# Attention stages of a fused transformer kernel: a fourth slot, row maxima and outputs turned through the score banks, outputs copied out by ScalarE and multiplied by GpSimd

## The reference

```python
x = x + _L1_attn_ref(_layernorm(x), ...)     # stage 4
    scores = jnp.einsum('bhqd,bhkd->bhqk', q, k) * scale
    attn = jax.nn.softmax(scores, axis=-1)
    out = jnp.einsum('bhqk,bhkd->bhqd', attn, v)
    return jnp.einsum('bld,ed->ble', out, wo) + bo
...
x = x + _L3_attn_ref(_layernorm(x), ...)     # stage 10
    att = (jnp.einsum('bhid,bhjd->bhij', q, k) + bias[None]) * (1.0 / math.sqrt(D))
    att = jax.nn.softmax(jnp.where(causal, att, -jnp.inf), axis=-1)
```

## Time and profile before

| | us |
|---|---|
| median of three runs | 3656.55 (3642.74 to 3657.66) |
| the profiled execution, its own time | 3656.68 |
| its span in the trace | 3654.9 |
| stage 4, about | 1074 to 1828 |
| stage 10, about | 2824 to 3410 |

### The profile page before, as it was taken

One profiled execution on the slowest core, in us unless ns is written; L12 is line 12 of the kernel. 1 busy time (PEld: TensorE's weight loads), 2 busy tenths in 40 slices (PEclk: granted clock), 3 DMA queues, 4 the chain that ended last, 5 costly groups with the idle time before them and its releaser, 6 DMA issues. The chain is left out here.

```text
span 3654.9 us, 60936 instructions
## 1 busy us (share of the span) xinstructions
PE 3204.0 (88%) x23629; PEld 1672.5 (46%) x23629; DVE 2528.7 (69%) x5604; ACT 1906.4 (52%) x3456; POOL 997.7 (27%) x858
## 2 busy tenths in 40 slices
PE   4678876798979999999889998989899799898899
PEld 3212223565652333333256666657676223232677
DVE  8787769777758888888487774363534688884433
ACT  2232222577757888888767773313222256677221
POOL 0245552667720000000096670000300211211100
PEclk9779978899987999999999998989999689899899
DMA  1000000211115000000021111000300500000100
GB/s 50 9 1 1 0 0 12 72 26 39 32 35 185 2 1 1 1 1 1 1 79 30 34 29 28 2 26 1 93 1 16 157 1 30 33 1 1 45 1 12
DMA packets 72854, 99.82 MB, mean 27 GB/s; under 512 B 11748, under 2 KB 51688, under 8 KB 72360
## 3 DMA queue, kind: packets, MB, share of 16 engines
q1 hardware_dynamic: 72568, 95.92, 8.9%
HBM read 62.81 MB, written 19.45 MB: 23 GB/s over the span
## 5 line engine op out<-in xcount | busy, mean ns | idle before, releaser
L1959 ACT ACTIVATE AR<-ps 128x1024 f32<-128x1024 f32 (+2 forms) x756 | 718.0, 995 | 194.8 <-PE ps L1860 122.9
L2042 DVE TENSOR_REDUCE AR<-ps 128x1 f32<-128x512 f32 x1056 | 671.7, 684 | 83.2 <-PE ps L1829 82.5
L1860 PE MATMUL ps<-AR 32*128 32x512 bf16 (+3 forms) x4992 | 610.2, 379 | 9.4 <-ACT AR L1959 5.8
L1829 PE MATMUL ps<-AR 32*128 32x512 bf16 (+3 forms) x1664 | 446.0, 400 | 41.0 <-DVE AR L2039 19.9
L1877 PE MATMUL ps<-AR 128*32 128x512 f32 (+3 forms) x3328 | 441.0, 603 | 4.0 <-ACT AR L1964 3.5
L2462 PEld LDWEIGHTS ps<-AR 128*128 128x128 f32 x3072 | 364.8, 193 | 60.5 <-issue 47.3
L2621 DVE SCALAR_TENSOR_TENSOR X<-ps,AR,X 128x128 f32<-128x128 f32 x512 | 143.6, 344 | 345.0 <-PE ps L2462 344.6
L2462 PE MATMUL ps<-AR 128*128 128x128 f32 x3072 | 364.9, 276 | 0.0
L1860 PEld LDWEIGHTS ps<-AR 32*128 32x128 bf16 x4992 | 227.2, 95 | 191.4 <-ACT AR L1959 47.6
L2437 PE MATMUL ps<-XT,AR 128*128 128x512 f32 x672 | 307.7, 594 | 0.0
L1829 PEld LDWEIGHTS ps<-AR 32*128 32x128 bf16 x1664 | 114.9, 92 | 396.0 <-DVE AR L2042 196.1
(11 more groups left out here) (324 smaller groups left out, 5711.2 us busy)
## 6 DMA issues: line engine op xcount, KB each, us to landing
AR<-AR SPq DMA_DIRECT2D x124, 128.0 KB, 2.3
AR<-in_c_rot SPq DMA_DIRECT2D x64, 128.0 KB, 2.2
AR<-in_L3f_w SPq DMA_DIRECT2D x30, 256.0 KB, 5.3
rows_KA<-AR SPq DMA_DIRECT2D x32, 128.0 KB, 2.4
AR<-scr_bias SPq DMA_DIRECT2D x32, 128.0 KB, 3.1
AR<-in_L2f_w SPq DMA_DIRECT2D x30, 128.0 KB, 2.8
AR<-rows_KC SPq DMA_DIRECT2D x7, 512.0 KB, 6.2
rows_QA<-AR SPq DMA_DIRECT2D x24, 128.0 KB, 2.4
```

The source lines that it names most:

```text
L1829: e.matmul(g.bank[b][:, 0:w], QA[rows, q, 128 * i:128 * i + 128], KA[rows, q, 512 * first:512 * first + w], start=way != "kept", stop=True ...
L1860: t = e.matmul(g.bank[h][:, lo:512], K[32 * h:32 * h + 32, q, 128 * kt:128 * kt + 128], Q[32 * h:32 * h + 32, q, queries], start=y == 0, s ...
L1959: e.activation(dst[:, :, lo:512], src[:, :, lo:512], ACT.Exp, scale=self.scale).then_inc(*s.up("exp" if u else "left", k, i, *((1,) if u e ...
L2042: e.tensor_reduce(o, g.bank[b][:, 0:w], AXX, ALU.max).then_inc(*s.up("reduced", k, n, h, st, kc))
```

## The change

1. `RC` gets a fourth slot in both stages; L1989 (and L2005 in stage 4) then waits for the part four before. Two of its slots serve later as `OS`.
2. In stage 4 only round 0 keeps the paired maxima. Head 1 of rounds 1 to 15 is reduced block by block like the others: 120 negated products, 120 copies of ACT and 120 paired reductions of DVE go, 240 plain reductions come. GpSimd negates once instead of 16 times. Within a "max" of round 0 the two products of one head now follow each other.
3. In stage 4 the maxima of a step stand in pairs: heads 2 and 3 ahead of the scores, heads 0 and 1 behind them. In stage 10 their order stays.
4. "max_rows" goes to bank 0 ahead of the scores u = 0 of a step, "finish" to bank 2 ahead of the scores u = 1. Both leave the ring.
5. The turned outputs are copied out of bank 2 by ACT ("finish", into `OS`); one step later DVE takes the reciprocal from there and GpSimd multiplies ("inverse").
6. In stage 10 the values' projections move from between the maxima of round 0 into the making of the parts.

```diff
-        self.RC = ar.f32(3, 512)
+        self.RC = ar.f32(4, 512)
+        self.OS = self.RC[:, 0:2, :]
...
-        if self.causal or (n and h != 1):
+        if self.causal or n:
             return "alone"
...
-    def plan_rows_max(self, n):
-        b = self.spare()
+    def plan_rows_max(self, n, b):
         self.plan.append(("max_rows", n, b, self.hold(b, ("max_row", n))))
 
-    def plan_finish(self, n):
-        b = self.spare()
-        self.plan.append(("finish", n, b, self.hold(b, ("finished", n))))
+    def plan_finish(self, n, b):
+        self.plan.append(("finish", n, b, self.hold(b, ("moved_out", n))))
...
+            if causal and x < len(self.parts) and not j:
+                self.plan_rows(c)
...
-        side = [0, 1, 2, 3]
+        side = [] if causal else [0, 1, 2, 3]
...
-            if self.rows_due:
-                self.plan_rows_max(self.rows_due.pop(0))
             self.plan_closed()
-        while self.rows_due:
-            self.plan_rows_max(self.rows_due.pop(0))
...
+            else:
+                order = [x[y] for y in range(3) for x in pairs if y < len(x)]
+                slots = [order[0:1], [], order[1:], []]
             for u in range(2):
                 for x in slots[u]:
                     self.plan_max(*x)
+                if u == 0 and self.rows_due:
+                    self.plan_rows_max(self.rows_due.pop(0), 0)
+                if u and finish_due:
+                    inverse_due += [(i + 1, finish_due[0])]
+                    self.plan_finish(finish_due.pop(0), 2)
...
+            if what == "finish":
+                n, b, _ = x
+                e.wait_ge(*s.at("o_turned", k, n))
+                if n > 1:
+                    e.wait_ge(*s.at("finished", k, n - 2))
+                e.activation(self.OS[:, n % 2, :], g.bank[b], ACT.Copy).then_inc(*s.up("ot", k, n, "out"))
...
-                if y > 2:
-                    e.wait_ge(*s.at("third", k, *self.parts[y - 3]))
+                if y > 3:
+                    e.wait_ge(*s.at("third", k, *self.parts[y - 4]))
...
+            if what == "inverse":
+                n = x[0]
+                gr, qc = self.rounds[n]
+                v = self.OS[:, n % 2, :].rearrange("p (i h d) -> p i h d", i=4, h=4)
+                e.wait_ge(*s.at("inverse", k, n))
+                e.tensor_tensor(self.AO[:, 4 * qc:4 * qc + 4, 32 * gr:32 * gr + 32].rearrange("p i (h d) -> p i h d", h=4),
+                                v[:, :, :, 0:8], bc(self.RD[:, n % 2, :, :], [128, 4, 4, 8], 3), ALU.mult).then_inc(
+                                    *s.up("finished", k, n))
```

More of the change, by code:

```diff
@@ L1454, in allocate @@
             self.KEPT = ar.f32(6, 512)
[L1455 removed]
+            self.NQ = ar.bf16(512)
         self.PB = ar.f32(4, 1024)
@@ L1608, in lay_plan @@
             pairs = [self.next_max(half, goal, 3) for half in (1, 0)]
-            order = [x[y] + (2 * x[y][1] + z,) for y in range(3) for x in pairs if y < len(x) for z in range(2)]
-            slots = [[x for y, x in enumerate(order) if 4 * y // max(4, len(order)) == z] for z in range(4)]
+            if causal:
+                order = [x[y] + (2 * x[y][1] + z,) for y in range(3) for x in pairs if y < len(x) for z in range(2)]
+                slots = [[x for y, x in enumerate(order) if 4 * y // max(4, len(order)) == z] for z in range(4)]
+            else:
+                order = [x[y] for y in range(3) for x in pairs if y < len(x)]
+                slots = [order[0:1], [], order[1:], []]
             for u in range(2):
@@ L1632, in lay_plan @@
                 self.plan_max(*x)
+            if inverse_due and inverse_due[0][0] == i:
+                self.plan.append(("inverse", inverse_due.pop(0)[1]))
             self.plan_closed()
@@ L1636, in lay_plan @@
         for n in finish_due + [15]:
-            self.plan_finish(n)
+            self.plan_finish(n, 2)
+            inverse_due += [(0, n)]
+        for _, n in inverse_due:
+            self.plan.append(("inverse", n))
     def wait_left(self, e, s, old):
@@ L1656, in wait_left @@
                 e.wait_ge(*s.at("max_row", k, *key))
-            if what == "finished":
-                e.wait_ge(*s.at("finished", k, *key))
+            if what == "moved_out":
+                e.wait_ge(*s.at("ot", k, *key, "out"))
             if what == "left":
@@ L1823, in tensor @@
                     if way == "kept":
-                        e.matmul(g.bank[b], self.NQ[rows, n % 2, 128 * st:128 * st + 128], KA[rows, q, chunk(kc)],
+                        e.matmul(g.bank[b], self.NQ[rows, 128 * st:128 * st + 128], KA[rows, q, chunk(kc)],
                                  start=True, stop=False, skip_group_check=True)
-                for h, b, old in heads:
-                    way, rows = self.way(n, h, kc), slice(32 * h, 32 * h + 32)
                     first = kc + 1 if way == "kept" else kc - 1 if way == "met" else kc
@@ L1911, in scalar @@
                     e.wait_ge(*s.at("rc_pool", k, c, j))
-                    e.activation(piece, self.RC[:, y % 3, :], ACT.Copy).then_inc(*s.up("piece", k, c, j, 1))
+                    e.activation(piece, self.RC[:, y % 4, :], ACT.Copy).then_inc(*s.up("piece", k, c, j, 1))
                 else:
@@ L2091, in gpsimd @@
         for what, *x in self.plan:
-            if what == "max" and not self.causal:
-                n, st, kc, heads = x
-                if n + st + kc == 0 and heads[0][0] == 2:
-                    self.turn_sign(e, s, 0)
-                if heads[0][0] == 2 and st == 3 and kc == (0 if n else 2) and n < 15:
-                    self.turn_sign(e, s, n + 1)
             if what == "compact" and self.causal:
                 y, c, j, _, _, _ = x
-                rest = self.RC[:, y % 3, :]
+                rest = self.RC[:, y % 4, :]
                 e.wait_ge(*s.at("rotated", k, c, j, 1))
@@ L2105, in gpsimd @@
                 e.wait_ge(*s.at("piece", k, c, j, 2))
-                e.tensor_tensor(self.P[:, j, 2, chunk(c)], self.RC[:, y % 3, :], self.P[:, j, 1, chunk(c)],
+                e.tensor_tensor(self.P[:, j, 2, chunk(c)], self.RC[:, y % 4, :], self.P[:, j, 1, chunk(c)],
                                 ALU.subtract).then_inc(*s.up("third", k, c, j))
+                if not self.causal and y == len(self.parts) - 1:
+                    e.wait_ge(*s.at(self.max_rows_in(*self.rounds[0], False), k))
+                    e.tensor_scalar(self.NQ, self.rows["QA"][:, 0, chunk(self.rounds[0][1])], -1.0, 1.0, ALU.mult,
+                                    ALU.mult).then_inc(*s.up("minus", k))
             if what == "close":
@@ L2648, in gpsimd @@
             root(e, s, g, k + 1, c)
-VECTOR = ("added", "below", "bias_rows", "biased", "centered", "closed", "final", "finished", "gate_added", "gated",
+VECTOR = ("added", "below", "bias_rows", "biased", "centered", "closed", "final", "gate_added", "gated",
           "hidden", "lifted_scores", "moments", "norms", "over", "p_odd", "product",
@@ L2658 @@
           "weights", "xh", "xt", "yt")
-GPSIMD = ("b2_added", "half", "last", "m_parts", "minus", "near_biased", "paired", "power", "product_pool", "rc_pool",
+GPSIMD = ("b2_added", "finished", "half", "last", "m_parts", "minus", "near_biased", "paired", "power", "product_pool", "rc_pool",
           "rest", "root", "rstd", "scaled_table", "summed", "third", "unit", "x_biased")
```

42 lines of the change are left out of this document (14 added, 28 removed).

## The result

| | before | after |
|---|---|---|
| median, us | 3657.11 (3642.74 to 3661.61, 4 runs) | 3759.70 (3753.42 to 3765.89, 4 runs) |
| span of the profiled execution | 3654.9 | 3751.6 |
| ratio after to before | | 1.0287, 95% interval 1.0254 to 1.0321 |

The changed kernel is slower by 103 us where +44 was forecast. I cut the two traces at the same places and took the difference of each piece (after less before, us): stage 4, up to its last projection, +24.8; stages 5 to 9, which nobody touched, and the start of stage 10 up to its first scores, -7.5, of which the start alone is -10.1 and the rest +2.7; the rounds of stage 10, from the first load of the values' weights to the last, **+78.4**; the end +1.4. With -0.4 between the first scores of stage 10 and its first values that is the 96.7 by which the spans differ. So nearly all of the surprise is in the rounds of stage 10.

A forecast was written before the change was run, and what follows sets the result against it. PE was taken as the bound, stretched by waits on the ring of three banks, where the fourth maximum waits for the first's reduction. Stage 4 +33 and stage 10 +11 on 3656.7 gave 3701 us; 8-in-10 range 3645 to 3765.

The forecast's parts named there:

- The plain steps: Stage 4 steps without turnings: every one 2.49 us instead of some at 2.61, saving 1.0 us a round.
- Turning steps of stage 4: Stage 4: row-maxima step 5.01 us against 3.79, output step 3.98 against 3.36, reciprocal +0.15 after; +14 us over 14 rounds.
- The clock in stage 4: Low-clock stretches from PE idling at turnings, about 1.5 us each, in 60% of 14 rounds: +13 us.
- The start of stage 10: First scores of stage 10 come earlier, limited by SP's load moving only 1 us: -11 us.
- I take +0.8 for each of 15: Stage 10 row-maxima turnings: +12 us together, each from 0 to +2.0, the latter as the bare chain would give.
- +0.5 each for 15, less DVE's shorter share: Stage 10 rounds, turning the outputs ahead of the second scores: +4 us together.
- DVE has three in the ring to work on: Stage 10 steps with many maxima: DVE has three in the ring to work on; row-maxima turnings taken at +0.8 us each.
- DVE as the bound: Rival, 8%: DVE's four reductions at 0.685 us each make a step 2.74 us, +58, total 3759.
- my signs of being wrong: Wrong if turning steps stay under 4.3 us or plain steps leave 2.49 by over 0.05.
- The rival of the low clock that doesn't come: Rival, 15%: no added low clock in either stage, so 13 and 5 us fall away, total 3683.
- the hidden turning: Rival, 10%: the close is done before its step, scores start at 1.64 instead of 2.81; total 3667.
- the faster case: Rival, 8%: turnings cost what they did because the ring, rid of both, gives back the scores' loss; total 3637.

The follow-up runs named there:

- The one loop: Against a kernel with both turnings still in the ring, PE sends a two-head max's first product before waiting for the second bank; 3627.18 us against 3642.54.
- filled: Changed kernel plus eight extra 128x512 products on PE while it waits at the turning of the row maxima; 3725.65 us, ratio 1.0188.
- filled_both: Changed kernel plus extra products on PE at the turnings of row maxima and, twelve of 128x128, of outputs; 3699.10 us, ratio 1.0123.
- outs_in_bank2: Changed kernel, but the row maxima are turned in the ring behind the scores as before; 3683.53 us, ratio 1.0081.

## Why the prediction was wrong in size

**The plain steps: right.** Forecast 2.49, all alike; 2.48. But the reason was half right. I credited the absent ACT release with it, and took the order of maxima and of PE's two products to be of no weight. The one loop was needed: without it the step is 2.58, longer than the mean before.

**Turning steps of stage 4: right.** Forecast 5.01 and 3.98, +0.15 in the step behind; measured 4.81 at the full clock, 4.03, and 2.64 behind the M step. I had put this 0.15 behind the F step, for the reciprocal; there the steps are 2.48 and 2.50, so that cause is wrong, and the one behind the M step I didn't single out. Less six low stretches of 1.4 (below) the fourteen rounds are 12.4 us longer, against 14; a round at the full clock goes from 42.95 to 43.78, +0.83 where +1.0 was forecast.

**The clock in stage 4: right price, fewer cases.** A low stretch costs 1.43 us (5.46 + 3.42 against 4.81 + 2.64 in the first one), forecast 1.5; it came in 6 of 14 rounds, not in 60%. Rounds +21.0, forecast +27. Start and end together took 4 us where 6.2 were forecast (and the start's terms, 1.0 + 2 x 0.6 + 1, make 3.2, not the 3.5 put down). Stage 4: +24.8 for +33.

**The start of stage 10: right.** SP's load moved to 2893.68, or 0.6 later in its stage than before (forecast 1), and the first scores are 10.1 nearer (forecast 11).

**The rounds of stage 10: here it failed.** The steps "I take +0.8 for each of 15" and "+0.5 each for 15, less DVE's shorter share" stood for +16, and the clock for +5; together 21, and the trace has 78.4. For the chain I took a value near the lower end of my own range (0 to 2.0) for the sake of a cover that isn't there: "DVE has three in the ring to work on". DVE works these off in the time in which PE waits for the close, and then waits itself. The step of 3263.24 shows +1.68 for the chain alone, near the bare chain's +2.0, and all 14 in filled, with their next steps, +1.54 each. At the outputs I had +0.5; here is a step at the full clock in both kernels, first before, then after (from:to as in rows 1), and two rows of the latter:

```profile
3280.73:3283.69 2.96, 2.87 (x31) 1.20 (x29) 2.75 (x11) 2.96 (x5) 0.00 (x0) 1.00 0.00 0
```
```profile
3356.75:3361.01 4.26, 2.90 (x30) 1.20 (x28) 2.31 (x10) 3.45 (x5) 0.00 (x0) 1.00 0.00 0
```
```profile
3358.95 0.63 PE L1891 MATMUL ps<-C,AR 128*128 128x128 f32 x4 [0.67 <-ACT AR L1973]
...
3360.26 0.39 PE L1865 MATMUL ps<-AR 32*128 32x512 bf16 x2 [0.69 <-ACT AR L1979]
```

That is +1.30; PE waits for both of ACT's copies. The one other such pair at the full clock goes from 3.91 to 4.14, +0.23 only; over all 14 the F steps of filled_both with their next have +1.26 each. With the 33 to 44 us of the clock (an estimate), for which I had said 5, this is the miss. The end of my range for the clock was 15. The stage already ran at 0.88 of it in the mean before the change; the stretch that I had shown, 0.98, was among its best, not its mean. Why the turnings brought 125 us of low clock to the rounds of stage 10 and only 25 to those of stage 4, no run shows.

**Why the total lies in the range all the same.** 3759.7 is 5 us below its upper end, which was made for DVE as the bound. That rival is out: DVE's start-to-start time within a step stayed at 0.60 and the plain steps at 2.48. The range held for a reason that wasn't the right one, which is luck; the narrower range that I gave my own forecast, 3680 to 3735, did not hold. None of my signs of being wrong came true either, since both were set for stage 4 (turning steps under 4.3, plain steps off 2.49 by over 0.05), and the miss is in stage 10. The rival of the low clock that doesn't come is out, and so are the hidden turning and the faster case: the first scores wait 0.69 for the copy, and the turning ahead of it 1.44 in stage 4 and 2.14 in the step of stage 10. The ring, rid of the row maxima, gave nothing back: the plain steps of stage 10 take 2.81 in the changed kernel and 2.78 in outs_in_bank2, which has them in the ring.

## What to carry to other kernels

A short dependent chain over four engines (DVE reduces, GpSimd splits, PE transposes, ACT copies) should not stand ahead of the big independent batch of products while its inputs are still being made: here the two turnings cost 121 us more ahead of the scores, in a bank that the scores need next. Behind the batch, PE makes scores in the time in which it would wait. If the chain must stand ahead, its inputs should have been made a step earlier; that alone gave back 71 of the row maxima's 76 us. When a price is taken within a range, ask whether the cover runs during the wait or has already run before it; and take the clock of a stage as its mean over all of its rounds, not from a stretch that reads well.

## What was unexpected

Extra products, whose results nobody reads, made the changed kernel 61 us faster: with PE idle less, the rounds of stage 10 spend 83 us at 1.2 GHz in place of 250. The price of low clock there was 0.26 us for each us of it. A second wait ahead of a first product, 0.10 us a step in the trace, was worth 15 us of the median (3642.5 to 3627.2); the removal of 120 copies and 120 paired reductions alone was worth nothing (3635.7 to 3642.5). And the start of stage 10 gave 20 us of the median where its chain is 7.4 to 10 shorter; where the rest comes from stays open.
